# Fused window attention and top-2 expert layer: projections, exponentials and rotations in another order, and another end phase

## The reference, cut to what matters

```python
qkv = ln(x) @ W_qkv + b_qkv
q, k = rope2(q), rope2(k)
attn = softmax(q * 8**-0.5 @ k.T + mask)        # per window of 64 and head
x = x + roll(attn @ v) @ W_proj + b_proj
t = ln(x)
probs, idx = top_k(softmax(t @ router_w.T), 2)
gates = probs / (sum(probs) + 1e-9)
h = silu(t @ w1[e].T) * (t @ w3[e].T)           # hidden size 682
out = x + sum over the two experts e of gates[e] * (h @ w2[e].T)
```

## Time and profile before

| | |
|---|---|
| median of 3 runs | 697.98 us (696.06 to 703.49) |
| the profiled execution | 693.54 us |
| its span | 691.2 us |
| TensorE busy | 593.7 us (86%) |
| VectorE busy | 484.2 us (70%) |
| GpSimd busy | 440.0 us (64%) |
| ScalarE busy | 414.2 us (60%) |

### The profile page before, as it was taken

One profiled execution on the slowest core, in us unless ns is written; L12 is line 12 of the kernel. 1 busy time (PEld: TensorE's weight loads), 2 busy tenths in 40 slices (PEclk: granted clock), 3 DMA queues, 4 the chain that ended last, 5 costly groups with the idle time before them and its releaser, 6 DMA issues.

```text
span 691.2 us, 20144 instructions
## 1 busy us (share of the span) xinstructions
PE 593.7 (86%) x5359; PEld 368.5 (53%) x5359; DVE 484.2 (70%) x1692; ACT 414.2 (60%) x934; POOL 440.0 (64%) x398
## 2 busy tenths in 40 slices
PE   1888888888888888852889999999999999999991
PEld 0466566656665556542445555555555555555550
DVE  2578878888878767763556667777676777776772
ACT  1678777778767767641345556555565565565560
POOL 1111777767767766546557876775766868666776
PEclk9999999999999999965599999999999999999996
DMA  9900000100000000001143444444434434344342
GB/s 328 295 10 9 26 27 25 33 25 25 25 24 25 24 23 24 26 25 37 45 85 39 53 43 44 50 41 48 50 38 50 44 43 52 38 50 48 38 52 16
DMA packets 85590, 34.67 MB, mean 50 GB/s; under 512 B 81966, under 2 KB 82478, under 8 KB 85038
## 3 DMA queue, kind: packets, MB, share of 16 engines
q0 software_dynamic: 26640, 9.90, 15.0%
q1 hardware_dynamic: 58910, 24.30, 14.3%
HBM read 20.21 MB, written 13.76 MB: 49 GB/s over the span
## 4 chain that ended last, share of the span: by engine, by line
PE 51%; issue 7%; DMA 5%; POOL 5%; DVE 4%; POOLq 1%; ACT 1%; DVEq 0%; ACTq 0%
PE bank L504 21%; PE bank L518 13%; POOL expert_rows L1225 3%; PE bank L473 3%; DMA expert_rows<-rows,slot_u 3%; PE bank L451 2%; PE bank L509 2%; PE bank L441 2%; PE bank L463 2%; PE bank L634 2%; DMA out<-y_early,meta 1%; PE bank L528 1%; DMA out<-y_out,token 1%; DVE smax L960 1%; PE bank L435 1%
## 5 line engine op out<-in xcount | busy, mean ns | idle before, releaser
L1313 POOL DMA_INDIRECT out<-y_out,token x144 | 222.8, 1547 | 89.2 <-DVE y_out L1136 53.1
L1225 POOL DMA_INDIRECT expert_rows<-rows,slot_u x144 | 147.8, 1027 | 79.2 <-issue 27.5
L504 PE MATMUL bank<-xs,w_sb 64*128 64x384 f32 x510 | 182.2, 500 | 4.7 <-DVE hid L1175 1.8
L505 PE MATMUL bank<-xs,w_sb 64*128 64x384 f32 x510 | 182.5, 501 | 0.0
L779 ACT ACTIVATE gate_h<-bank 128x384 f32<-128x384 f32 x255 | 125.2, 492 | 61.2 <-PE bank L505 43.6
L1175 DVE TENSOR_TENSOR hid<-gate_h,bank 128x384 f32<-128x384 f32 x255 | 140.4, 554 | 30.2 <-ACT gate_h L779 13.2
L504 PEld LDWEIGHTS bank<-xs,w_sb 64*128 64x128 f32 x510 | 92.0, 189 | 88.2 <-issue 39.4
L518 PE MATMUL bank<-hid,w_sb 128*64 128x384 f32 x612 | 110.5, 496 | 2.7 <-DVE hid L1175 2.7
L505 PEld LDWEIGHTS bank<-xs,w_sb 64*128 64x128 f32 x510 | 92.0, 189 | 0.0
L789 ACT ACTIVATE y_odd<-bank 64x384 f32<-64x384 f32 x51 | 24.9, 487 | 85.9 <-PE bank L518 82.0
L1168 DVE TENSOR_TENSOR y_t<-y_odd,bank 64x384 f32<-64x384 f32 x51 | 27.8, 546 | 56.3 <-ACT y_odd L789 53.4
(11 more groups left out here) (136 smaller groups left out, 977.2 us busy)
## 6 DMA issues: line engine op xcount, KB each, us to landing
xin<-expert_rows SPq DMA_DIRECT2D x51, 99.0 KB
xin<-expert_rows SPq DMA_DIRECT2D x51, 96.0 KB
w_sb<-w SPq DMA_DIRECT2D x1, 3072.0 KB, 22.1
out<-res_all SPq DMA_DIRECT2D x18, 128.0 KB
expert_rows<-rows,slot_u POOLq DMA_INDIRECT x144
out<-y_out,token POOLq DMA_INDIRECT x144
x_all<-x_win SPq DMA_DIRECT2D x1, 1664.0 KB, 8.6
res_all<-x_res SPq DMA_DIRECT2D x1, 1664.0 KB, 12.1
```

Source lines behind the costliest of these rows:

```text
L504: pe.matmul(ps_h[c % RING], w13_sb[0:C, e, c, :], xs[0:C, :], start=True, stop=True)
L505: pe.matmul(ps_g[c % RING], w13_sb[C:2 * C, e, c, :], xs[C:2 * C, :], start=True, stop=True).then_inc(s_h, 1)
L1225: pool.indirect_dma_start(rows_dram, bass.IndirectOffsetOnAxis(ap=slot_u[:, spar, i // 2, i % 2:i % 2 + 1], axis=0), rows[:, spar, i // 2, ...
L1313: pool.indirect_dma_start(out, bass.IndirectOffsetOnAxis(ap=token[:, c:c + 1], axis=0), y_out[:, c, :], None, compute_op=ALU.add).then_inc ...
```

## The change

It has five parts.

- TensorE: v is projected for `att_g` at the start of the next body, behind the scores of the first pair, no longer at the end of its own body. The scores of the second pair and the projection of q and k move: the pair stands behind att's transposes, then q and k, then the weighing of tile 0.
- ScalarE: tile 0's exponential is the first instruction of the body, ahead of the copy of tile 3's turned probabilities and of x.
- VectorE: the rotation of q follows that of k directly, and tile 3's softmax stands ahead of the residual add.
- End phase: the counting of tiles is one comparison with a table of 24 bounds per expert and a sum instead of shifts and multiplications; expert 0 has four early tiles, and four tiles have buffers of their own; GpSimd scatters a group's eight blocks without the wait in the middle, and in the first draining body both roots that are left stand there: one behind two scatters, the last one behind all eight, where it takes the place of the wait.
- The constants have 606 columns instead of 422.

```diff
-EARLY = (1, 1, 1, 0, 0, 0)
-OWN = 3
+EARLY = (1, 1, 1, 0, 0, 0, 0)
+OWN = 4
...
@@ tensor, body
                 if ok(att_g):
                     scores(att_g, 0, masked)
+                if ok(att_g):
+                    after(pe, s_qst, att_g, -(G - 1))
+                    hold(pe)
+                    for w in range(2 * G):
+                        for half in range(2):
+                            own = slice(half * C, (half + 1) * C)
+                            mm = pe.matmul(ps_v[own, w * C:(w + 1) * C], xt[own, w * N:(w + 1) * N], wqkv_sb[own, W_V:W_V + C], start=True, stop=True)
+                    mm.then_inc(s_v, G)
...
                 if ok(att_g):
-                    if isinstance(b, int) and b == G:
-                        pe.wait_ge(s_biased, 1)
-                    scores(att_g, 1, masked)
                     turn_probs(att_g, 0)
...
                 if ok(att_g):
-                    weigh_values(att_g, 0)
-
+                    if isinstance(b, int) and b == G:
+                        pe.wait_ge(s_biased, 1)
+                    scores(att_g, 1, masked)
                 if ok(b):
...
                     pe.matmul(ps_k, wqkv_sb[C:2 * C, W_QK:W_QK + P], xt[C:2 * C, :], start=True, stop=True).then_inc(s_qk, G)
+                if ok(att_g):
+                    weigh_values(att_g, 0)
+
...
@@ scalar, body
+                if ok(att_g):
+                    exponent(att_g, 0)
                 if ok(b - LAG_PT):
                     keep_turned(b - LAG_PT, 3)
...
                 if ok(att_g):
-                    exponent(att_g, 0)
                     after(act, s_v, att_g, -(G - 1))
...
@@ vector, body
                     rotate(b, ps_k, k_st, 1, rope_k, s_kst, s_sum, b - G)
+                if ok(b):
+                    rotate(b, ps_q, q_st, 0, rope_q, s_qst, s_score, b - G)
                 if ok(new):
                     ln1_squares(new)
+                if ok(att_g):
+                    soften(att_g + 3, 3)
                 if ok(out_g):
                     after(dve, s_proj, out_g, -(G - 1))
...
-                if ok(b):
-                    rotate(b, ps_q, q_st, 0, rope_q, s_qst, s_score, b - G)
...
-                if ok(att_g):
-                    soften(att_g + 3, 3)
...
@@ vector, tile count
-            dve.tensor_copy(cnt_f[:], ps_cnt).then_inc(s_tstep, 1)
+            dve.tensor_tensor(padrow_f[:], ps_cnt, late_base[:], ALU.add).then_inc(s_tstep, 1)
             dve.wait_ge(s_tstep, 1)
...
+            dve.tensor_tensor(over[:], padrow_f[:].unsqueeze(2).to_broadcast([P, E, MOST]), tile_ends, ALU.is_gt).then_inc(s_tstep, 1)
+            dve.tensor_copy(padrow_i[:], padrow_f[:])
             dve.wait_ge(s_tstep, 2)
+            dve.reduce_sum(til_m[:], over[:], AX).then_inc(s_tstep, 1)
             dve.wait_ge(s_tstep, 3)
...
@@ gpsimd, draining bodies
-                    scatter(to, (0, 1, 2, 3), par)
-                    pause(send, par, 4)
-                    scatter(to, (4, 5), par)
-                    if ok(out_g):
+                    scatter(to, (0, 1), par)
+                    if b == TILES:
                         root(ln2_rstd, ln2_vare, s2vare, s2rstd, s2xn, out_g)
-                    scatter(to, (6, 7), par)
-                    pause(send, par, 8)
+                    scatter(to, range(2, 2 * G), par)
+                    if b == TILES:
+                        root(ln2_rstd, ln2_vare, s2vare, s2rstd, s2xn, out_g + G)
+                    else:
+                        pause(send, par, 2 * G)
```

More of the change, by code:

```diff
@@ L71 @@
 BIG = -1.0e30
-THIRD, THIRD_SHIFT = 171, 9
-assert SUB == 3 and all(x * THIRD >> THIRD_SHIFT == x // SUB for x in range(TOKENS // P + SUB + 1))
+MOST = TOKENS // SLOTS
+assert MOST * SLOTS == TOKENS
 MASKED_PER_IMAGE = PER_IMAGE // 3
@@ L90 @@
 FIRST_TILES = 5 * G
-K_IDENT, K_ROPE, K_SUM, K_HEAD, K_VMASK, K_IOTA, K_BASE, K_SKIP, K_TIL = 0, 128, 256, 384, 388, 390, 398, 406, 414
-K_COLS = 422
+K_IDENT, K_ROPE, K_SUM, K_HEAD, K_VMASK, K_IOTA, K_BASE, K_SKIP, K_ENDS = 0, 128, 256, 384, 388, 390, 398, 406, 414
+K_COLS = 414 + E * MOST
 W_QK, W_V, W_BIAS, W_VBIAS = 0, 128, 192, 194
@@ L132, in build @@
         early_rows = consts[:, K_SKIP:K_SKIP + E]
-        tile_base = consts[:, K_TIL:K_TIL + E]
+        tile_ends = consts[:, K_ENDS:K_ENDS + E * MOST].rearrange("p (e t) -> p e t", e=E)
         ident_b = constb[:, B_IDENT:B_IDENT + P]
@@ L189, in build @@
         late_base = sb("late_base", [P, E])
-        cnt_f = sb("cnt_f", [P, E])
-        cnt_i = sb("cnt_i", [P, E], I32)
-        til_i = sb("til_i", [P, E], I32)
-        til_s = sb("til_s", [P, E], I32)
-        til_f = sb("til_f", [P, E])
+        over = sb("over", [P, E, MOST])
         til_m = sb("til_m", [P, E])
@@ L627, in body @@
                     turn_probs(att_g + 2, 2)
-                if ok(b):
-                    after(pe, s_qst, b, -(G - 1))
-                    hold(pe)
-                    for w in range(2 * G):
-                        for half in range(2):
-                            own = slice(half * C, (half + 1) * C)
-                            mm = pe.matmul(ps_v[own, w * C:(w + 1) * C], xt[own, w * N:(w + 1) * N], wqkv_sb[own, W_V:W_V + C], start=True, stop=True)
-                    mm.then_inc(s_v, G)
             groups(pe, body, by_pairs=False)
@@ L1075, in _ @@
             dve.wait_ge(s_cnt, 1)
-            dve.tensor_copy(cnt_f[:], ps_cnt).then_inc(s_tstep, 1)
+            dve.tensor_tensor(padrow_f[:], ps_cnt, late_base[:], ALU.add).then_inc(s_tstep, 1)
             dve.wait_ge(s_tstep, 1)
-            dve.tensor_tensor(padrow_f[:], cnt_f[:], late_base[:], ALU.add).then_inc(s_tstep, 1)
+            dve.tensor_tensor(over[:], padrow_f[:].unsqueeze(2).to_broadcast([P, E, MOST]), tile_ends, ALU.is_gt).then_inc(s_tstep, 1)
+            dve.tensor_copy(padrow_i[:], padrow_f[:])
@@ L1079, in _ @@
             dve.wait_ge(s_tstep, 2)
-            dve.tensor_tensor(til_f[:], padrow_f[:], tile_base, ALU.subtract).then_inc(s_tstep, 1)
+            dve.reduce_sum(til_m[:], over[:], AX).then_inc(s_tstep, 1)
             dve.wait_ge(s_tstep, 3)
-            dve.tensor_copy(til_i[:], til_f[:]).then_inc(s_tstep, 1)
-            dve.tensor_copy(padrow_i[:], padrow_f[:]).then_inc(s_tstep, 1)
+            dve.tensor_tensor_scan(ends_f[:], til_m[:], zero8[:], float(len(EARLY)), ALU.add, ALU.add).then_inc(s_tstep, 1)
@@ L1084, in _ @@
+            dve.wait_ge(s_tstep, 4)
+            dve.tensor_scalar(ends_mf[:], ends_f[:], float(-BEHIND), None, ALU.add).then_inc(s_tstep, 1)
             dve.wait_ge(s_tstep, 5)
-            dve.tensor_scalar(til_s[:], til_i[:], P.bit_length() - 1, None, ALU.arith_shift_right).then_inc(s_tstep, 1)
-            dve.wait_ge(s_tstep, 6)
-            dve.tensor_copy(til_f[:], til_s[:]).then_inc(s_tstep, 1)
-            dve.wait_ge(s_tstep, 7)
-            dve.tensor_scalar(til_m[:], til_f[:], float(THIRD), None, ALU.mult).then_inc(s_tstep, 1)
@@ L1101, in _ @@
-            dve.tensor_tensor_scan(ends_f[:], til_m[:], zero8[:], float(len(EARLY)), ALU.add, ALU.add).then_inc(s_tstep, 1)
-            dve.wait_ge(s_tstep, 13)
-            dve.tensor_scalar(ends_mf[:], ends_f[:], float(-BEHIND), None, ALU.add).then_inc(s_tstep, 1)
-            dve.wait_ge(s_tstep, 14)
             dve.tensor_copy(ends_m[:], ends_mf[:])
@@ L1390, in constants @@
     kf[:, K_SKIP:K_SKIP + E] = SKIP
-    kf[:, K_TIL:K_TIL + E] = np.arange(E) * REGION + np.array(SKIP) - (SLOTS - 1)
+    ends = (np.arange(E) * REGION + np.array(SKIP))[:, None] + np.arange(MOST)[None, :] * SLOTS
+    ends[:, 0] = -1
+    kf[:, K_ENDS:K_ENDS + E * MOST] = ends.reshape(-1)
     kb = np.zeros((P, B_COLS), np.float32)
```

9 lines of the change are left out of this document (removed).

## The result

730.75 us median (728.41 to 733.70, 4 runs) against 697.02 (693.83 to 703.49, 4 runs) of the kernel before beside it: a ratio of 1.049, with its 95% interval in brackets: [1.045, 1.053]. The forecast was 706.5, its range 690 to 713; the loss is four times the one I worked out, and outside the range.

What follows compares the result with a forecast made beforehand. The order in which VectorE and TensorE wait for each other bounds the attention group. Ring 4.0, clock 5.0, slow part 0, constants 0.3, end -0.8: +8.5 us on 693.54, 702.0, plus 4.4 for the runs' median: 706.5, range 690 to 713.

Steps and rivals of the forecast that it cites:

- The rotation of q ... and tile 3's softmax ... go in front of the residual add: VectorE's attention loop: some 2.0 us move into the 1.90 us stall, so tile 0's softmax starts 1.4 us earlier.
- the turn ends at +8.2 as before: TensorE in the attention loop: tile 3's turn ends 8.2 us after k's rotation, unchanged by v's new place.
- The order on ScalarE costs the gain and a little more: Attention loop: exponential ahead of the copy puts the reciprocal at +10.9 against +10.44; 0.44 us more per group, 4.0 in nine.
- The ring: Attention group: closed chain of waits between engines; the exponential holds the copy, weighing and reciprocal wait, 15.66 us instead of 15.22.
- the clock's term: TensorE in the fast part: half clock returns in most groups, 0.55 us each, 9 x 0.55 = 5.0 us.
- A granted share clearly under 1.00 before 178 us: Sign in the changed profile: TensorE's clock falls in the fast attention part too; the forecast falls if it stays 1.00.
- The slow part, priced at 0: Attention from 178.88 to 280.87 us: new groups take 17.0 us as before, so no change.
- shorter ring: Rival, attention loop: exponential does not hold the copy, reciprocal at +9.7 or sooner, groups 14.5 us, 681 us; chance 0.12.
- End phase: End of attention and expert tiles: 8 us won, mostly lost again in VectorE's wait on adds; -0.8 us, bounds -1.8 and +1.5.
- The one wait of 7 to 8 us on an add's landing: Sign in the expert tiles: VectorE waits once for 7 to 8 us, TensorE idles and its clock falls.
- The constants: First loads: constants grow from 211 to 303 KB; +0.3 us, between 0 and 2.0.
- TensorE 1.3 for the copy: Sign in the attention loop: TensorE waits 1.3 us, before 0.59, for ScalarE's copy of turned probabilities.

Runs made afterwards that it cites:

- e16: Kernel before, with only GpSimd's wait for tile 3's softmax ahead of its fifth and sixth scatter taken out: 732.6 us, ratio 1.045.
- e4: Kernel before, with VectorE's new order alone (q's rotation and tile 3's softmax moved up): 720.2 us, ratio 1.034.
- e15: Kernel before, with VectorE's new order and GpSimd's fifth and sixth scatter waiting for the group's membership mask: 688.2 us, ratio 0.981.
- e14: Changed kernel, with GpSimd's fifth and sixth scatter waiting for the group's membership mask instead of tile 3's softmax: 738.3 us, 1.053 against before.
- e22: Changed kernel, with the scatters' later wait (membership mask), ScalarE's old order and v's projection back behind tile 2's turn: 675.9 us, 0.985 against before.
- e17: Changed kernel, with the scatters' later wait (membership mask) and v's projection back behind tile 2's turn: 705.8 us, 1.030 against before.
- e18: Kernel before, with only v's projection moved behind the next first scores: 692.6 us, ratio 1.009.
- e21: Changed kernel, with the scatters' later wait (membership mask) and ScalarE's old order, v in its new place: 685.3 us, 1.002 against before.
- e1: Changed kernel, with ScalarE's old order (tile 0's exponential behind the copies of tile 3's probabilities and x): 734.4 us, 1.053 against before.
- e3: Kernel before, with the changed kernel's end phase, tile counts, early tiles and constants alone: 693.3 us, ratio 0.999.
- e8: Changed kernel, with TensorE's looped attention groups written out, so without its loop branch: 737.1 us, 1.046 against before.
- e9: Kernel before, with VectorE's new order alone and TensorE's looped groups written out: 723.0 us, ratio 1.031.

## Why the prediction was wrong

**The step that failed first: "The rotation of q ... and tile 3's softmax ... go in front of the residual add".** I counted what VectorE does behind it and what TensorE waits for, but not who else waits on the softmax's semaphore. GpSimd does, ahead of its fifth scatter; I wrote of GpSimd in the end phase alone. With that wait satisfied early the scatters run together and TensorE runs dry: +4.5% with nothing else changed (e16), +3.4% with VectorE's order (e4), -1.9% when the distance is kept (e15). The forecast has no term for it, nor has a rival. The row of before quoted above shows the wait, and the view of GpSimd's waits from 60 to 300 us (in total, times, longest) sums it up:

```profile
POOL expert_rows L1225 <- DVE probs L963: 16.4, 15, 2.0
```

This step by itself, and the next two together without it, each bring a loss of the whole's kind: 1.034 with VectorE's order and its spells (e4), 1.053 without spells but with TensorE's and ScalarE's orders (e14), 1.049 with everything. The costs overlap, so no fixed share of the 33.7 us belongs to one of them; with all three undone the changed kernel is faster than before (e22).

**Second: "the turn ends at +8.2 as before".** v was said to take the place ahead of the turn that it had behind the turn of tile 2. But in the old place it ran in the time in which the scores wait for the logits' copy, which stands behind k's masked copies on ScalarE (in e17 v starts at 131.12, the copy at 131.30, the scores at 132.49, 0.22 behind v); in the new one TensorE waits for that copy with nothing to do (9.0 us in 9 instances from 60 to 300 us, up to 1.5) and then does scores and v one behind the other. That holds where q's rotation is early: in before v itself waited for q, and there its move cost only 0.9% (e18). Priced at 0; e21 against e22 puts it at 1.7%, e14 against e17 at 2.3%.

**Third, right in kind and too small: "The order on ScalarE costs the gain and a little more".** I had the reciprocal at +10.9 instead of +10.44, 0.44 us a group, and 0.55 for the clock. Without spells and with v in its old place it is 17.12 us a group (six from 75.10 to 177.82, e17) against 15.44 (e22) and 15.54 (before): 1.6 to 1.7 us, where my two terms made 1.0. The ring itself was as drawn: the copy held by the exponential, TensorE waiting (1.98, forecast 1.3), VectorE waiting ahead of the reciprocal (1.72, forecast 1.5 to 1.9), the half clock behind it falling on pair 1's scores. Mis-sized is the clock's term: I had let most of the half clock fall into 1 us of spare time. But the scores that it stretches from 1.09 to 1.99 us stand ahead of q and k, and the time from the reciprocal to the next rotation, 4.78 in the forecast, is 5.68 in six groups of e17. That the changed kernel itself does not react to ScalarE's order (e1) is no contradiction: there the dry spells and v make the turn late, and the copy would come no sooner (in the group shown it waits 1.48 us for the turn, until 160.92).

**The clock.** "A granted share clearly under 1.00 before 178 us" came: 0.80. In e17, where only this ring is new, it is 0.89. The Trainium skill (TensorE: Matmul & The Clock Gate, "A second HAM failure mode") says of another kernel that frequent short idle spells between groups of matmuls make the clock swing between its two levels; the traces agree, with 2.90 busy of 4.60 us ahead of 10 us at half speed. The slow part, priced at 0, lost 5.4 us (107.35 instead of 101.99 for its six groups), the fast part 24.0 and the groups ahead of it 4.0.

**The case "shorter ring".** The walk along VectorE itself was right: I had the first maximum at +4.63 and tile 0's softmax at +7.4, and in the group of e22 from 117.22 they start at +4.63 (121.85) and +7.47 (124.69). So the case was killed by the scatters, by v's place and by ScalarE, not by the logits. Even so it was priced too high: with all that undone the reciprocal comes at +9.5 to +9.7 in six of e22's seven fast groups, as the case has it, but the next rotation mostly follows 5.4 to 5.7 us behind instead of 4.78, and the group takes 15.44, not 14.5.

**End phase, right in its sum.** e3 shows it alone: the last root at 320.40, not the 317.5 that I gave, but sooner than the 324.29 of before; the first early add at 357.58 instead of 359.39, 1.8 us where I had 3; 0.999 in all. What is won ahead of that add goes again behind it: from there to the end of the span e3 takes 334.7 us, before 331.8, the changed kernel 336.3. In the changed kernel the first early add (393.11) is as late as the loop (33.7 against 33.4 us). The one wait of 7 to 8 us on an add's landing that I named as a sign did not come: VectorE's longest wait there (7.4 us) is for ScalarE's `y_odd`, and comes with the new end phase (6.7 us in e3). The constants: 303 KB landed in 4.9 us instead of 4.6, the 0.3 of the sum.

**Signs.** No idle time ahead of the residual add: right. 1.5 to 1.9 ahead of the reciprocal, rotations 15.7 to 17 apart: of the right kind, too small. TensorE 1.3 for the copy: in the changed kernel 5.6 us in 9 instances, 0.6 on average and up to 1.8, because the turn ahead of the copy is late itself. The last root: 355.13, where 317.5 and the loop's 33.4 make 350.9.

## What to carry to other kernels

Before an instruction is moved, list everyone who waits on its semaphore, the engines that "bound nothing" too: a wait whose operands the waiting engine does not need is a pace, and whoever moves its source changes the pace. When two costs hide each other, undoing one shows nothing (e1, e14); undo them together and then one at a time. A block of work that looks movable may be what fills a wait, and has its price where it leaves.

## What the hardware showed that I had not expected

Indirect scatters issued back to back by GpSimd (each 0.96 us, 0.30 apart) go with spells in which TensorE starts one or two products every 0.74 us for 2 to 3 us, in the dense stretch of small products (v, scores, weighing), and in which VectorE waits 2 us for a semaphore of products already issued. Such a semaphore can be 1.5 us late without a dry spell too (e15). The first three scatters of a group follow each other just as closely in every kernel here, without products 0.74 us apart: they fall on a stretch with fewer and longer products (L608, L614 in before). In e3 even eight in a row (333.67 to 343.47) do without them, beside the long products of the expert tiles (L500, L501); two gaps of 0.48 and 1.15 us stand there for which the trace names no releaser. It is not TensorE's branch (e8, e9), and the DMA engines are not busy: their share in e9 from 148.50 to 151.50 us, the spell, is 0.20 at most in any half microsecond. Which resource the two share stays open; no run separated the number of scatters in a row from the stretch of TensorE that they meet.
